# A delta-rule layer with experts: the gated output's scaling on ScalarE, the queries' square sums by products into ones, and the order around them

## The chip, the cores and the metric

One core of a Trainium2 chip runs the whole program in one launch. Its engines are TensorE (PE in the profile, its weight loads PEld), VectorE (DVE), ScalarE (ACT), GpSimd (POOL) and SyncE (SP, which here only issues DMAs). The metric is the device time of one execution in microseconds; less is better. Each engine runs its own list of instructions in order, and semaphores order the engines among themselves. All orders are written out by hand in the kernel.

## The reference

The input is 4 sequences of 512 tokens with 256 features. Two layers follow. Layer 0 adds to the tokens the sum of a gated delta-rule attention (32 value heads, 16 key heads, 128 wide) and a mixture of 64 experts; layer 1 adds a small attention over the 4 sequences and 8 experts. The part that matters here, cut down:

```python
y = conv(x @ w_qkv)                       # causal, 4 taps, per channel
q, k, v = split(silu(y))
q = q / sqrt(sum(q * q) + 1e-6) * DK ** (-0.5)
k = k / sqrt(sum(k * k) + 1e-6)
# for each token: Sm = Sm * exp(g); delta = (v - k @ Sm) * beta; Sm += outer(k, delta); o = q @ Sm
og = o * silu(z)
var = mean(og * og)
on = og * rsqrt(var + EPS) * norm_w
out = on @ w_out
```

## The kernel before, in words

`build_program` runs three parts: layer norm, gates and routing; then `heads_and_experts`, which holds the change; then the experts' combination and layer 1.

`heads_and_experts` makes 64 steps (STEPS): 16 key heads, and for each 4 chunks of 128 tokens, for all 4 sequences at once. So a tile of a step is 128 partitions by 512 columns. A step g belongs to chunk g % 4; `first_chunk` has no earlier state, so it has no `residual`, `queries_state` and `keys_state`, and `last_chunk` needs no `state_update`. The work of one chunk is spread over three steps (step g does the projections and products of chunk g, part of the triangular inverse of chunk g-1, and solves, outputs and state of chunk g-2). On the same step runs one unit of the experts (EX_IN, EX_GATE, EX_UP, EX_DOWN; in the first 8 steps GpSimd scatters tokens by indirect DMAs instead, and the experts' units begin at step 9).

The order on each engine is the function `step(g)` of its block:

- TensorE (L1002): `project` (L789) multiplies the tokens with the weights of one channel type into one of two PSUM tiles `psF`, which are used in turn in the order PLACES (L399); `slot_free` (L772) waits until ScalarE or VectorE has drained the use before. `turn_keys` (L825) and `turn_queries` (L829) transpose the keys and queries after the convolution; `products` (L837) makes k·k and q·k; `solve`, `within`, `state_update` (L935 to L963) serve chunk g-2; `turn_out` (L965) transposes the scaled output and `project_out` (L972) multiplies it with `w_out`.
- VectorE (L1603): `conv` (L1408) makes three of the four taps of the convolution, each a multiply-add over 128x512; `key_scales` (L1436), `decayed_products` (L1453, from PSUM), `row_scales` (L1553, the inverse roots), `decays` (a scan, L1444), `pivots` (L1465, the first part of the inverse of the 16x16 blocks), `level`, `new_state`, `gather_out`.
- ScalarE (L1278): `evacuate` (L1131) drains a projection; `silu`; `squares` (L1159) reads the turned keys or queries from PSUM, with an accumulated sum of each of the 4 blocks; `w_copy` (L1236), `values` (L1183, drains the turned values), `keys_copy` (L1169), `out_squares` (L1242), `compact`, `inverse_copy`, `silu_z`, `out_turned` (L1249).
- GpSimd (L1776): `join` (L1704, the second part of the blocks' inverse, after `pivots`), `gated` (L1738, o times silu(z)), `rho_w`, `state_decay`, `normed` (L1745, the gated output times its inverse root), `hidden`, `mask`, `next_weights`, and the scatters.
- SyncE loads the decays, weights and experts and carries the blocks' DMAs. Its list is not touched.

The orders of the uses of `psF` for `filled` and `drained` (L403) are not touched either. After step 63 a tail follows in which the last chunks and the last 9 experts' units run.

## Time and profile before

| what | value |
|---|---|
| median of 3 runs | 2678.14 us (2676.47 to 2680.68) |
| the profiled execution's own time | 2679.44 us |
| its span, first to last instruction | 2677.7 us |
| TensorE, VectorE busy | 88%, 87% of the span |
| ScalarE, GpSimd busy | 67%, 53% |
| mean granted TensorE clock | 0.958 of full |

The span is the profiled execution's stretch from the first to the last instruction; its own time is 1.7 us longer, and 1.3 us above the median. Busy time is the union of an engine's instructions. A busy share says nothing about which wait ends last; for that the timelines of one step are read side by side. The page's chain of the work that ended last covers mostly the last part of the program.

### The profile page before, as it was taken

The numbers are of one execution on the slowest core, as the hardware profiler recorded it, in microseconds if no ns is written. First come the engines' busy times: TensorE is split into PE (matmuls) and PEld (weight loads), VectorE is DVE, ScalarE is ACT, GpSimd is POOL, SyncE is SP. The second block draws the span as 40 slices with busy tenths as digits, with TensorE's granted clock in tenths as the row PEclk, the third lists the DMA queues.
The fourth block names the chain that finished last, engine by engine and source line by source line (L and its number), as shares of the span: only waits on it lengthen the run. The fifth ranks groups of instructions, "written<-read, shape, count | busy, mean of one in ns | idle before, by whom it ended". The sixth has DMA issues, their size and how long they took to land. (4 is left out here: it accounts for less than half of the span.)

```text
span 2677.7 us, 74015 instructions
## 1 busy us (share of the span) xinstructions
PE 2362.6 (88%) x27695; PEld 1951.4 (73%) x27696; DVE 2326.0 (87%) x5305; ACT 1788.2 (67%) x5621; POOL 1424.9 (53%) x1368
## 2 busy tenths in 40 slices
PE   1477889999999999999999999999999999758998
PEld 1366777888787878787878787878787878635555
DVE  7677888999999999999999999999999998289996
ACT  1356767787878787878787878787877787412121
POOL 2388885555555555555555555555555555266510
PEclk8679899999999999999999999999999999869999
DMA  5232112212222222221222222212122112263311
GB/s 208 89 94 67 41 42 61 57 50 51 55 57 50 57 50 57 49 57 49 57 50 57 50 57 50 57 49 58 49 57 49 46 49 57 64 206 106 104 59 48
DMA packets 244701, 175.39 MB, mean 66 GB/s; under 512 B 152635, under 2 KB 212714, under 8 KB 243160
## 3 DMA queue, kind: packets, MB, share of 16 engines
q1 hardware_dynamic: 221543, 136.89, 19.1%
q0 software_dynamic: 12288, 24.19, 2.9%
q10 hardware_dynamic: 10512, 9.57, 1.1%
q8 instruction: 222, 3.64, 0.6%
q14 instruction: 136, 1.11, 0.1%
HBM read 126.88 MB, written 53.08 MB: 67 GB/s over the span
## 5 line engine op out<-in xcount | busy, mean ns | idle before, releaser
L1417 DVE SCALAR_TENSOR_TENSOR p_y<-p_xr,cw,p_y 128x512 f32<-128x512 f32 x768 | 760.3, 997 | 33.2 <-ACT p_y L1141 14.4
L798 PE MATMUL p_psF<-xnS,w_hl 128*128 128x512 f32 x1536 | 430.6, 416 | 20.4 <-PEq L651 11.1
L798 PEld LDWEIGHTS p_psF<-xnS,w_hl 128*128 128x128 f32 x1536 | 274.4, 192 | 85.9 <-DVE p_ATP L1461 11.4
L1710 POOL TENSOR_TENSOR p_terms<-p_U 64x512 f32<-64x512 f32 x64 | 130.8, 2043 | 335.8 <-DVE p_U L1486 335.7
L1461 DVE SCALAR_TENSOR_TENSOR p_ATP<-p_psF,p_sj,p_E 128x256 f32<-128x256 f32 x512 | 211.0, 477 | 65.8 <-PE p_psF L844 64.2
L1749 POOL TENSOR_TENSOR p_O<-p_OG,p_sm 128x512 f32<-128x512 f32 x128 | 155.7, 1239 | 195.0 <-DVE p_sm L60 171.8
L1743 POOL TENSOR_TENSOR p_OG<-p_O,p_zs 128x512 f32<-128x512 f32 x128 | 162.6, 1271 | 140.5 <-ACT p_ktok L1172 69.3
L979 PE MATMUL p_psO<-p_wout,p_ont 128*128 128x256 f32 x1024 | 235.3, 383 | 0.1
L1712 POOL TENSOR_TENSOR p_terms<-p_terms 64x256 f32<-64x256 f32 (+1 forms) x256 | 220.0, 859 | 20.1
L1138 ACT ACTIVATE p_xr<-p_psF 128x512 f32<-128x512 f32 x256 | 153.4, 599 | 93.6 <-PE p_psF L798 81.8
L813 PEld LDWEIGHTS p_psF<-w_hl,xnS 128*128 128x128 f32 x1536 | 200.1, 189 | 14.3 <-DVE p_ATP L1461 5.1
L979 PEld LDWEIGHTS p_psO<-p_wout,p_ont 128*128 128x128 f32 x1024 | 191.4, 192 | 25.2 <-ACT p_ont L1253 0.8
L1246 ACT ACTIVATE p_O<-p_OG 128x128 f32<-128x128 f32 x512 | 152.4, 308 | 82.4 <-POOL p_OG L1743 81.7
L813 PE MATMUL p_psF<-w_hl,xnS 128*128 128x256 f32 x1536 | 206.0, 284 | 0.0
L1141 ACT ACTIVATE p_y<-p_psF,cw 128x512 f32<-128x512 f32 x256 | 175.0, 684 | 0.8
L1166 ACT ACTIVATE p_y<-p_psF 128x128 f32<-128x128 f32 x512 | 137.1, 300 | 48.2 <-PE p_psF L822 48.2
L822 PE MATMUL p_psF<-ident,p_kq 128*128 128x128 f32 x512 | 86.1, 292 | 93.7 <-ACT p_kq L1151 93.5
L1451 DVE TENSOR_TENSOR_SCAN p_E<-p_ab,p_identr 128x512 f32<-128x512 f32 x128 | 160.6, 1255 | 8.2 <-DMA p_ab<-decays 8.2
L1966 POOL DMA_INDIRECT w_hl<-expert_out,slot_u x96 | 100.8, 1050 | 86.9 <-DVE acc L2211 36.2
L1189 ACT ACTIVATE p_vs<-p_psF,p_vsc 128x128 f32<-128x128 f32 x512 | 146.2, 379 | 0.0
L822 PEld LDWEIGHTS p_psF<-ident,p_kq 128*128 128x128 f32 x512 | 54.8, 143 | 124.1 <-ACT p_kq L1151 124.1
L844 PE MATMUL p_psF<-p_kq 128*128 128x256 f32 x512 | 138.1, 395 | 5.5 <-ACT p_y L1166 5.5
(337 smaller groups left out, 6153.8 us busy)
## 6 DMA issues: line engine op xcount, KB each, us to landing
p_ab<-decays SPq DMA_DIRECT2D x64, 512.0 KB, 5.5
w_raw<-in_w_in SPq DMA_DIRECT2D x16, 768.0 KB, 4.0
p_wgu<-in_w_gu SPq DMA_DIRECT2D x60, 176.0 KB
expert_out<-p_ye ACTq DMA_DIRECT2D x73, 128.0 KB, 1.7
expert_in<-p_zero SPq DMA_DIRECT2D x16, 512.0 KB, 7.5
blocks_out<-p_ATc SPq DMA_DIRECT2D x64, 128.0 KB
p_DTc<-blocks_back SPq DMA_DIRECT2D x64, 128.0 KB
p_xe<-expert_in SPq DMA_DIRECT2D x60, 128.0 KB
```

Source lines behind the costliest of these rows:

```text
L798: m = pe.matmul(b4(psF[f % 2][:, :]), w_hl[:, wp, kt, ty * P:(ty + 1) * P], xnS[:, xp, kt, :].rearrange("p (b t) -> p b t", b=B)[:, :, c * ...
L813: m = pe.matmul(psF[f % 2][:, (b % 2) * 2 * P:(b % 2 + 1) * 2 * P], xnS[:, xp, kt, b * S + c * P:b * S + (c + 1) * P], w_hl[:, wp, kt, 4 * ...
L979: m = pe.matmul(psOO[:, b * D:(b + 1) * D], ont[:, v, b, :], wout[:, v, :], start=(v == 0), stop=(v == 1))
L1138: act.activation(xr[:, ty, :, TAPS - 1:], b4(psF[f % 2][:, :]), ACT.Copy)
L1141: act.activation(y[:, ty, :, :], b4(psF[f % 2][:, :]), ACT.Copy, scale=cw[:, ty, TAPS - 1:TAPS]).then_inc(s["drained"], 1)
L1246: m = act.activation(O1[:, v, b, :], OG[:, v, b, :], ACT.Square, accum_out=so[:, v, b:b + 1])
L1417: m = dve.scalar_tensor_tensor(y[:, ty, :, :], xr[:, ty, :, tap:tap + P], cw[:, ty, tap:tap + 1], y[:, ty, :, :], ALU.mult, ALU.add)
L1451: dve.tensor_tensor_scan(flat(E[:, v, :, :]), flat(ab[:, v, :, :]), flat(identr[:, :, :]), 0.0, ALU.mult, ALU.add).then_inc(s["scan"], 1)
L1461: m = dve.scalar_tensor_tensor(ATP[g % 2][:, v, b, :, :], psF[f % 2][:, (b % 2) * 2 * P:(b % 2 + 1) * 2 * P].rearrange("p (u t) -> p u t", ...
L1712: link(pool.tensor_tensor(terms[:, 0:k, :, :], terms[:, 0:k, :, :], terms[:, k:2 * k, :, :], ALU.add))
L1743: pool.tensor_tensor(OG[:, v, :, :], O1[:, v, :, :], zs[g % 2][:, v, :, :], ALU.mult).then_inc(s["og"], 1)
L1749: pool.tensor_tensor(O1[:, v, :, :], OG[:, v, :, :], over(sm[:, 1, 1 + v, :]), ALU.mult).then_inc(s["on"], 1)
```

## The change

- `normed` moves from GpSimd (two tensor-tensor products of 128x512) to ScalarE (eight ACTIVATEs of 128x128 with a per-partition scale), behind `evacuate(g, 2)`.
- The queries' square sums: instead of transposing the queries on TensorE and squaring them from PSUM with an accumulated sum, ScalarE squares the queries in place (one ACTIVATE of 128x512, `query_squares`), TensorE multiplies each of the 4 blocks into a column of ones (`query_norms`), and ScalarE copies the 128x4 sums (`query_sums`).
- The key scales: a tensor-scalar and a tensor-tensor become two scalar-tensor-tensor instructions, with a tile of 1e-6 and a factor of 1.
- Orders. ScalarE: `silu(g, 1)` ahead of `values(g-1, 0)` and `keys_copy`; `level5` ahead of `silu(g-1, 2)`; `normed`, then `inverse_copy`; `spread`, `halves` and `inverse_copy(g-1, 5)` ahead of `silu(g, 3)`. TensorE: EX_IN ahead of `within(g-2, 1)`; `state_update(g-2, 1)` behind `level_y`; `project(g, 2)` ahead of `level_x`; EX_UP ahead of `turn_out`. VectorE: both `history` and both `decays` ahead of `pivots`; `row_scales`, `conv(g, 3)` ahead of `rows_decay` and `output_weights`. GpSimd: `gated(g-2, 1)` ahead of two scatters; `mask` ahead of `hidden`.

The tail (after step 63) gets the same orders; its lines are left out here.

```diff
--- before
+++ after
@@ -420,7 +420,7 @@
 
 
 
-PER = dict(hist=2, silu=2, silu_v0=1, silu_v1=1, kss=1, vsc=1, s_ready=1, scan=2, rho=1, atp=4,
+PER = dict(hist=2, silu=2, squared=1, silu_v0=1, silu_v1=1, kss=1, vsc=1, s_ready=1, scan=2, rho=1, atp=4,
            compact=4, masked=1, halved=2, pivoted=1, joined=1, spread=4, t5=3, tt=1,
            ks=2, r=2, qs=2, qg=2, w=2, wsb=2, wr=2, decayed=2, o=2, o1=2, su=2, st=2, og=2, so=2, rstd=1, on=2, ot=2, ont=2, outp=1, acc=1)
 PER_UNIT = dict(hh=1)
@@ -475,7 +475,8 @@
         ss = [sb(f"ss{p}", [P, 2, B]) for p in range(2)]
         sm = sb("sm", [P, 3, 3, B])
         n2 = sb("n2", [P, B])
-        scratch = sb("scratch", [P, 1])
+        floor = sb("floor", [P, B])
+        ones = sb("ones", [P, 1])
         vsc = sb("vsc", [P, B])
         sj = sb("sj", [P, B, 2])
         xq = [sb(f"xq{p}", [P, B]) for p in range(2)]
@@ -651,10 +652,12 @@
         with nc.Block() as block:
             @block.vector
             def _(dve):
-                for t in (xr[:, :, :, 0:TAPS - 1], scratch[:, :], D64X[:, :, :, :], TT[0][:, :, :, :]):
+                for t in (xr[:, :, :, 0:TAPS - 1], D64X[:, :, :, :], TT[0][:, :, :, :]):
                     dve.memset(t, 0.0).then_inc(init, 1)
+                dve.memset(ones[:, :], 1.0).then_inc(init, 1)
+                dve.memset(floor[:, :], 1e-6).then_inc(init, 1)
                 dve.tensor_copy(identr[:, :, :], ident[:, :].unsqueeze(1).to_broadcast([P, B, P])).then_inc(init, 1)
-                dve.wait_ge(init, 8)
+                dve.wait_ge(init, 9)
 
             @block.gpsimd
             def _(pool):
@@ -826,9 +829,13 @@
                 wait(pe, "silu", g, 1)
                 turn(g, KEYS_T, lambda b: kq[g % 2][:, b, K_, :])
 
-            def turn_queries(g):
-                wait(pe, "silu", g, 2)
-                turn(g, QUERIES_T, lambda b: kq[g % 2][:, b, Q_, :])
+            def query_norms(g):
+
+                slot_free(g, QUERIES_T)
+                wait(pe, "squared", g, 1)
+                for b in range(B):
+                    m = pe.matmul(psF[QUERIES_T % 2][:, b:b + 1], y[:, 1, b, :], ones[:, :], start=True, stop=True)
+                m.then_inc(s["filled"], 1)
 
             def turn_values(g, v):
                 wait(pe, ("silu_v0", "silu_v1")[v], g, 1)
@@ -1017,28 +1024,28 @@
                     solve(g - 2, 0)
                     solve(g - 2, 1)
                     within(g - 2, 0)
+                expert(g, EX_IN)
+                if g >= 2:
                     within(g - 2, 1)
-                expert(g, EX_IN)
-                turn_queries(g)
+                query_norms(g)
                 products(g, 0)
                 if g >= 2:
                     state_update(g - 2, 0)
                 products(g, 1)
-                if g >= 2:
-                    state_update(g - 2, 1)
                 project(g, 3)
                 project_z(g, (0, 1))
                 expert(g, EX_GATE)
+                project(g, 2)
                 if g >= 1:
                     level_x(g - 1, 4)
-                project(g, 2)
                 project_z(g, (2, 3))
+                expert(g, EX_UP)
                 if g >= 2:
                     turn_out(g - 2)
                 if g >= 1:
                     level_y(g - 1, 4)
-                expert(g, EX_UP)
                 if g >= 2:
+                    state_update(g - 2, 1)
                     project_out(g - 2, (0, 1))
                     project_out(g - 2, (2, 3))
                 if g >= 1:
@@ -1136,6 +1143,8 @@
                     act.wait_ge(cw_in, g // NC)
                 wait(act, "hist", g - 1, 1 + ty // 2)
                 act.activation(xr[:, ty, :, TAPS - 1:], b4(psF[f % 2][:, :]), ACT.Copy)
+                if ty == Q_:
+                    wait_filled(act, g - 1, QUERIES_T)
                 if ty >= 2:
                     wait_filled(act, g - 1, VALUES_T[ty - 2])
                 act.activation(y[:, ty, :, :], b4(psF[f % 2][:, :]), ACT.Copy, scale=cw[:, ty, TAPS - 1:TAPS]).then_inc(s["drained"], 1)
@@ -1156,15 +1165,23 @@
                 wait(act, "og", g - 2, 2)
                 act.activation(zs[g % 2][:, :, 2 * half:2 * half + 2, :], psF[f % 2][:, :].rearrange("p (b v t) -> p v b t", b=2, v=2), ACT.Silu).then_inc(s["drained"], 1)
 
-            def squares(g, u):
-
-                p, f = g % 2, (KEYS_T, QUERIES_T)[u]
-                wait_filled(act, g, f)
-                if u == 0:
-                    wait(act, "vsc", g - 2, 1)
+            def key_squares(g):
+
+                wait_filled(act, g, KEYS_T)
+                wait(act, "vsc", g - 2, 1)
                 for b in range(B):
-                    m = act.activation(y[:, u, b, :], psF[f % 2][:, b * P:(b + 1) * P], ACT.Square, accum_out=ss[p][:, u, b:b + 1])
-                m.then_inc(s["drained" if u else "kss"], 1)
+                    m = act.activation(y[:, 0, b, :], psF[KEYS_T % 2][:, b * P:(b + 1) * P], ACT.Square, accum_out=ss[g % 2][:, 0, b:b + 1])
+                m.then_inc(s["kss"], 1)
+
+            def query_squares(g):
+
+                wait(act, "silu", g, 2)
+                act.activation(y[:, 1, :, :], kq[g % 2][:, :, Q_, :], ACT.Square).then_inc(s["squared"], 1)
+
+            def query_sums(g):
+
+                wait_filled(act, g, QUERIES_T)
+                act.activation(ss[g % 2][:, 1, :], psF[QUERIES_T % 2][:, 0:B], ACT.Copy).then_inc(s["drained"], 1)
 
             def keys_copy(g):
                 wait_filled(act, g, KEYS_T)
@@ -1245,6 +1262,15 @@
                 for b in range(B):
                     m = act.activation(O1[:, v, b, :], OG[:, v, b, :], ACT.Square, accum_out=so[:, v, b:b + 1])
                 m.then_inc(s["so"], 1)
+
+            def normed(g):
+                wait(act, "rstd", g, 1)
+                wait(act, "so", g, 2)
+                for v in range(2):
+                    wait(act, "og", g, v + 1)
+                    for b in range(B):
+                        m = act.activation(O1[:, v, b, :], OG[:, v, b, :], ACT.Copy, scale=sm[:, 1, 1 + v, b:b + 1])
+                    m.then_inc(s["on"], 1)
 
             def out_turned(g, v):
                 if v == 0:
@@ -1278,9 +1304,10 @@
             def step(g):
                 if g >= 1:
                     expert(g - 1, EX_DOWN)
-                    silu(g - 1, 2)
                 if g >= 2:
                     level5(g - 2)
+                if g >= 1:
+                    silu(g - 1, 2)
                 evacuate(g, 0)
                 if g >= 2:
                     queries(g - 2, 0)
@@ -1291,16 +1318,17 @@
                 silu(g, 0)
                 if g >= 2:
                     queries(g - 2, 1)
-                squares(g, 0)
+                key_squares(g)
                 if g >= 2:
                     w_copy(g - 2, 0)
                     w_copy(g - 2, 1)
+                silu(g, 1)
                 if g >= 1:
                     values(g - 1, 0)
                 keys_copy(g)
-                silu(g, 1)
+                query_squares(g)
                 expert(g, EX_IN)
-                squares(g, 1)
+                query_sums(g)
                 if g >= 2:
                     out_squares(g - 2, 0)
                     out_squares(g - 2, 1)
@@ -1308,22 +1336,23 @@
                 silu_z(g, 0)
                 expert(g, EX_GATE)
                 compact(g)
+                evacuate(g, 2)
+                if g >= 2:
+                    normed(g - 2)
                 if g >= 1:
                     inverse_copy(g - 1, 4)
-                evacuate(g, 2)
                 silu_z(g, 1)
-                if g >= 2:
-                    out_turned(g - 2, 0)
                 if g >= 1:
                     store_expert(g - 1)
                 if g >= 2:
+                    out_turned(g - 2, 0)
                     out_turned(g - 2, 1)
                 expert(g, EX_UP)
+                if g >= 1:
+                    spread(g - 1)
+                    halves(g - 1)
+                    inverse_copy(g - 1, 5)
                 silu(g, 3)
-                if g >= 1:
-                    halves(g - 1)
-                    spread(g - 1)
-                    inverse_copy(g - 1, 5)
             for g in range(STEPS):
                 step(g)
 
@@ -1437,9 +1468,9 @@
 
                 h = 2 * (g // NC)
                 wait(dve, "kss", g, 1)
-                link(dve.tensor_scalar(sm[:, 0, 0, :], ss[g % 2][:, 0, :], 1e-6, None, ALU.add))
+                link(dve.scalar_tensor_tensor(sm[:, 0, 0, :], ss[g % 2][:, 0, :], 1.0, floor[:, :], ALU.mult, ALU.add))
                 link(dve.reciprocal(n2[:, :], sm[:, 0, 0, :]))
-                dve.tensor_tensor(sj[:, :, :], gates[:, 0, g % NC:NT:NC, h:h + 2], n2[:, :].unsqueeze(2).to_broadcast([P, B, 2]), ALU.mult).then_inc(s["s_ready"], 1)
+                dve.scalar_tensor_tensor(sj[:, :, :], gates[:, 0, g % NC:NT:NC, h:h + 2], 1.0, n2[:, :].unsqueeze(2).to_broadcast([P, B, 2]), ALU.mult, ALU.mult).then_inc(s["s_ready"], 1)
 
             def decays(g, v):
 
@@ -1601,23 +1632,23 @@
                     dve.tensor_copy(cw[:, :, :], cw_raw[:, :, :]).then_inc(cw_in, 1)
 
             def step(g):
+                if g >= 1:
+                    history(g - 1, 0)
                 decays(g, 0)
                 if g >= 3:
                     gather_out(g - 3)
-                if g >= 1:
-                    history(g - 1, 0)
                 if g >= 2:
                     residual(g - 2, 0)
                 if g >= 1:
+                    history(g - 1, 1)
+                decays(g, 1)
+                if g >= 1:
                     pivots(g - 1)
-                decays(g, 1)
                 conv(g, 0)
                 if g >= 2:
                     level6(g - 2)
                     residual(g - 2, 1)
                 conv(g, 1)
-                if g >= 1:
-                    history(g - 1, 1)
                 if g >= 2:
                     outputs(g - 2, 0)
                 key_scales(g)
@@ -1627,20 +1658,21 @@
                 decayed_products(g, 1)
                 if g >= 1:
                     turn_cores(g - 1)
-                output_weights(g)
-                rows_decay(g)
                 row_scales(g)
                 conv(g, 3)
+                next_weights(g, 0)
                 conv(g, 2)
+                rows_decay(g)
+                next_taps(g)
+                output_weights(g)
                 if g >= 1:
                     level(g - 1, 4)
-                next_taps(g)
-                next_weights(g, 0)
-                next_weights(g, 1)
                 if g >= 2:
                     new_state(g - 2, 0)
+                next_weights(g, 1)
+                next_weights(g, 2)
+                if g >= 2:
                     new_state(g - 2, 1)
-                next_weights(g, 2)
             for g in range(STEPS):
                 step(g)
 
@@ -1742,12 +1774,6 @@
                 wait_drained(pool, g, Z1)
                 pool.tensor_tensor(OG[:, v, :, :], O1[:, v, :, :], zs[g % 2][:, v, :, :], ALU.mult).then_inc(s["og"], 1)
 
-            def normed(g):
-                wait(pool, "rstd", g, 1)
-                for v in range(2):
-                    wait(pool, "og", g, v + 1)
-                    pool.tensor_tensor(O1[:, v, :, :], OG[:, v, :, :], over(sm[:, 1, 1 + v, :]), ALU.mult).then_inc(s["on"], 1)
-
             def hidden(g):
 
                 if not in_use(g, EX_UP):
@@ -1780,29 +1806,27 @@
                 if g >= 2:
                     gated(g - 2, 0)
                     rho_w(g - 2)
+                    gated(g - 2, 1)
                 scatter(g, 1)
                 scatter(g, 2)
                 if g >= 2:
-                    gated(g - 2, 1)
                     state_decay(g - 2)
                 scatter(g, 3)
                 scatter(g, 4)
                 scatter(g, 5)
                 scatter(g, 6)
-                if g >= 2:
-                    normed(g - 2)
                 scatter(g, 7)
                 scatter(g, 8)
                 next_weights(g, 0)
                 scatter(g, 9)
+                scatter(g, 10)
+                mask(g)
+                scatter(g, 11)
                 hidden(g)
-                mask(g)
-                scatter(g, 10)
-                scatter(g, 11)
                 scatter(g, 12)
                 scatter(g, 13)
+                scatter(g, 14)
                 next_weights(g, 1)
-                scatter(g, 14)
                 next_weights(g, 2)
                 scatter(g, 15)
             for g in range(STEPS):
```

## Rows read from the trace of the kernel before

**Rows 1.** The page, part 1: busy us of each engine.

```profile
PE 2362.6 (88%) x27695; PEld 1951.4 (73%) x27696; DVE 2326.0 (87%) x5305; ACT 1788.2 (67%) x5621; POOL 1424.9 (53%) x1368
```
**Rows 2.** Busy time by stage: length; busy PE, PEld, DVE, ACT, POOL; granted clock; DMA share; GB/s.

```profile
898.60:1031.69 133.09, 125.92 (x1671) 107.98 (x1665) 122.42 (x265) 106.89 (x345) 71.66 (x69) 1.00 0.22 54
```
**Rows 3.** Waits from 760 to 1720 us: total us, times, longest.

```profile
PEld p_psF L822 <- ACT p_kq L1151: 49.6, 58, 2.1
...
DVE p_ATP L1461 <- PE p_psF L844: 18.8, 43, 0.9
```
**Rows 4.** Timeline of PE: start us, length us, instruction, count, [idle before, releaser].

```profile
906.16 0.65 PE L822 MATMUL p_psF<-ident,p_kq 128*128 128x128 f32 x4 [0.24 <-ACT p_kq L1151]
906.66 1.95 PE L943 MATMUL p_psS<-p_vs,p_TT 128*128 128x128 f32 x16
908.72 2.05 PE L953 MATMUL p_psO<-p_Ws,p_ATP 128*128 128x128 f32 x16
...
911.34 0.66 PE L822 MATMUL p_psF<-ident,p_kq 128*128 128x128 f32 x4 [0.34 <-ACT p_kq L1151]
...
913.16 1.16 PE L962 MATMUL p_psS<-p_Wr,p_ktok 128*128 128x128 f32 x8 [0.30 <-POOL p_Wr L1726]
914.15 1.03 PE L844 MATMUL p_psF<-p_kq 128*128 128x256 f32 x4
...
915.83 1.63 PE L798 MATMUL p_psF<-xnS,w_hl 128*128 128x512 f32 x6
...
922.94 1.04 PE L969 MATMUL p_psO<-ident,p_O 128*128 128x128 f32 x8
...
924.59 0.67 PE L996 MATMUL p_psF<-p_xeT,p_wgu 128*88 128x128 f32 x4
...
941.52 0.66 PE L822 MATMUL p_psF<-ident,p_kq 128*128 128x128 f32 x4 [1.88 <-ACT p_kq L1151]
...
1005.65 0.66 PE L822 MATMUL p_psF<-ident,p_kq 128*128 128x128 f32 x4 [1.16 <-ACT p_kq L1151]
```
**Rows 5.** Timeline of ACT, same step.

```profile
909.14 1.14 ACT L1189 ACTIVATE p_vs<-p_psF,p_vsc 128x128 f32<-128x128 f32 x4
...
910.62 0.67 ACT L1151 ACTIVATE p_kq<-p_y 128x512 f32<-128x512 f32 x1
...
915.42 0.31 ACT L1246 ACTIVATE p_O<-p_OG 128x128 f32<-128x128 f32 x1 [1.09 <-POOL p_OG L1743]
...
915.73 0.29 ACT L1246 ACTIVATE p_O<-p_OG 128x128 f32<-128x128 f32 x1
...
921.34 0.39 ACT L1196 ACTIVATE p_Xs<-p_psI 128x256 f32<-128x256 f32 x1
...
922.31 0.69 ACT L1141 ACTIVATE p_y<-p_psF,cw 128x512 f32<-128x512 f32 x1
```
**Rows 6.** Timeline of DVE, same step; last row: ns min/median/max of line 1417.

```profile
901.50 3.26 DVE L1417 SCALAR_TENSOR_TENSOR p_y<-p_xr,cw,p_y 128x512 f32<-128x512 f32 x3 [0.25 <-ACT p_y L1141]
...
906.61 2.57 DVE L1417 SCALAR_TENSOR_TENSOR p_y<-p_xr,cw,p_y 128x512 f32<-128x512 f32 x3
...
910.93 1.20 DVE L1442 TENSOR_TENSOR p_sj<-gates,p_n 128x8 f32<-128x8 f32 x1
...
915.22 1.66 DVE L1461 SCALAR_TENSOR_TENSOR p_ATP<-p_psF,p_sj,p_E 128x256 f32<-128x256 f32 x4 [0.67 <-PE p_psF L844]
...
919.49 3.00 DVE L1417 SCALAR_TENSOR_TENSOR p_y<-p_xr,cw,p_y 128x512 f32<-128x512 f32 x2
...
L1417 DVE SCALAR_TENSOR_TENSOR p_y<-p_xr,cw,p_y x342: 717/827/1554, 768.4 to 1710.1; 128x512 f32<-128x512 f32 x171
```
**Rows 7.** Timeline of POOL, same step.

```profile
907.91 0.65 POOL L1716 TENSOR_TENSOR p_U<-p_terms 64x64 f32<-64x64 f32 x1
910.84 1.27 POOL L1743 TENSOR_TENSOR p_OG<-p_O,p_zs 128x512 f32<-128x512 f32 x1 [2.28 <-ACT p_ktok L1172]
...
919.45 2.48 POOL L1749 TENSOR_TENSOR p_O<-p_OG,p_sm 128x512 f32<-128x512 f32 x2 [2.11 <-DVE p_sm L60]
```

28 lines of the change are left out of this document (14 added, 14 removed).

## The prediction

> **What bounds the kernel now.** I read the page's busy shares first, then the busy time by stage, then the waits, and last the timelines of one step. The page gives TensorE 2362.6 us, VectorE 2326.0, ScalarE 1788.2 and GpSimd 1424.9 of the span [rows 1]. The work repeats every four steps of a head, so I take the four steps from 898.60 to 1031.69 us: in 133.09 us TensorE is busy 125.92, VectorE 122.42, ScalarE 106.89, at a granted clock of 1.00 [rows 2]. So TensorE is idle 7.17 us in four steps, and no reordering can win more than that there. The waits say where: nearly all of it ends in `turn` (line 822, keys or queries from `kq`, released by ScalarE's silu), 49.6 us of weight loads from 760 to 1720 us. VectorE waits most for the products, 18.8 us [rows 3].
>
> The timeline of the step that begins at 898.60 shows two halves [rows 4]. In the first TensorE waits 0.24 us for the turned keys, 0.34 for the queries, 0.30 for `Wr`. From `project(g, 3)` at 915.83 to the end of the step it waits for nothing. `turn_out` starts at 922.94; GpSimd's `normed` ran from 919.45 for 2.48 us, so its result was 1.0 us early [rows 4, 7]. ScalarE's order decides the first half: after the second `w_copy` it does `values(g-1, 0)` (from 909.14), the keys' copy and only then silu of the queries at 910.62 [rows 5]. That silu's input, conv(g, 1), is ready at 909.18 [rows 6], so little is lost by the order.
>
> **The change part by part.**
>
> 1. *Key scales.* The TENSOR_TENSOR of 8 elements takes 1.20 us [rows 6]. It runs beside GpSimd's `gated` (910.84 + 1.27 = 912.11) and ends with it at 912.13 [rows 6, 7]. A SCALAR_TENSOR_TENSOR beside GpSimd is slowed but doesn't wait for the end: two taps of the convolution beside `normed` take 3.00 us together [rows 6]. I price the new form at 0.2 us, between that tiny size costing nothing and the full 1.20. VectorE wins 1.0 us, but just before `decayed_products`, where it waits for the products anyway [rows 3]; this gain is worth nothing unless the products come sooner.
>
> 2. *`normed` leaves GpSimd.* conv(g, 3) loses its neighbour. A tap free of GpSimd takes at best 0.72 us [rows 6], so two taps come down from 3.00 to about 1.5: 1.5 us off VectorE, in the second half, where TensorE doesn't wait for it. What it can buy is an earlier start of the next conv(g, 0). In the steps after a last chunk that matters: the turned keys come 1.88 us late there [rows 4].
>
> 3. *`normed` on ScalarE.* Eight ACTIVATEs of 128x128. The nearest, out of the same tile, stand 0.31 us apart with their accumulator read between (915.42 to 915.73) and four from PSUM take 1.14 us [rows 5]: 2.0 to 2.5 us, taken 2.3. They stand behind `evacuate(g, 2)`, which ends at 923.00 today [rows 5], and, without the 0.36 us of `inverse_copy` ahead of it, at 922.65. So the halves are ready at 923.8 and 924.95 on today's clock. TensorE, with EX_UP (0.6 us, line 996 [rows 4]) now ahead of `turn_out`, arrives at 923.55, turns one half in 0.5 and waits for the other: 0.25 + 0.7, about **1.0 us of new idle per step** (0.6 with the short price). `inverse_copy`, `silu_z` and `out_turned` follow while TensorE does `level_y` and the moved `state_update`, so `project_out` should just get its input.
>
> 4. *Query squares.* ScalarE drops four squares from PSUM and takes one of 128x512 and a tiny copy: a small relief. TensorE gives up four transposes (the next instruction starts 0.5 us after them: 906.66 - 906.16) for four products of one column, eight records. Bounds: at the pace of full 128x128 products 8/16 of 1.95 us = 1.0, and nothing [rows 4]. I take 0.5, since the weights are full and the columns few, so this changes nothing.
>
> 5. *What it waits for.* TensorE's `query_norms` stands ahead of both `products`, and needs the squares. ScalarE's new order is silu(g, 1), `values`, `keys_copy`, `query_squares`. Silu can't start before conv(g, 1) ends. That end moves: `pivots` now stands behind `decays(g, 1)` (1.2 us), so GpSimd's `join` (today until 908.56 [rows 7]) runs 1.2 us longer beside conv(g, 0) and conv(g, 1), whose taps it slows (3.26 and 2.57 us for three, against 2.2 at best [rows 6]). I take conv(g, 1) 0.5 us later, between 0 and 1.2. Then: silu 909.9 to 910.45, values to 911.45, keys_copy to 911.95, squares to 912.6. But EX_IN on TensorE needs the PSUM slot that `values` drains (911.5), and `within(g-2, 1)` (1.0 us) is queued behind it: EX_IN to 912.0, within to 913.0. So `query_norms` starts at **913.0 instead of 911.34**, 1.65 us late. Then 0.5 + 1.0 (products 0) + 1.0 (`state_update` 0) + 0.9 (products 1) gives `project(g, 3)` at 916.4, only 0.55 later than 915.83, because `state_update(g-2, 1)` has gone from here. `project_z` behind it waits for VectorE's second `decayed_products` (products 1 end 916.55, plus 1.66 [rows 6]): 918.2 against an arrival of 917.85, another 0.35.
>
> 6. *The moved `state_update(g-2, 1)`* comes back in the second half: eight records like those at 913.16, the next instruction 1.0 us later [rows 4], of which I count 0.9, the pace beside other products.
>
> 7. *Hidden:* the histories, `rows_decay`, `spread` before `halves`, `mask` before `hidden`. All have their readers over a microsecond later, and VectorE and ScalarE have spare time in the second half once TensorE is the late one; if not, they are worth 0.2 us each. In the first eight steps GpSimd also scatters; losing `normed` (2.5 us) could help there, 0 to 2.5 a step, taken at 1 for eight steps.
>
> **The sum.** This step: 0.55 + 0.35 + 0.9 + 1.0 = +2.8 us. The next (the one with 1.88 us of lateness, of which 1.6 goes, as VectorE is earlier): +1.2. The third has no `state_update`, so it loses the delay of 1.65 directly: +2.6. The fourth has no residual and less to wait for: +2.6. Together +9.2 on 133.09. Steps 9 to 63 are 13.75 such groups: +126 us; less 8 for the early steps: +118. On the profiled execution (span 2677.7, its own time 2679.44) that is 2797; on the median shown, 1.3 us lower, **2796 us**. With every term at its low bound (conv(g, 1) not delayed, norms free, `normed` 2.0) the four steps lose 5 to 6 and the time is 2745; at the high bounds (1.2 us, 1.0 us, 2.5 us) they lose 14 and it is 2860. For this case alone the range is 2745 to 2860.
>
> **The rivals.**
>
> *VectorE's relief decides (faster).* If VectorE is what really holds the loop, 2.5 us less work a step brings conv(g, 1) to its end a microsecond sooner. Then silu, `values` and squares are done before TensorE has finished `within`, and the waits at the turned keys close: these are 0.24, 1.88 and 1.16 us [rows 4] in three steps, the third repeats the 0.24: 3.5 us in four. That is 2.6%, up to 55 us: 2625; I put it at 2640 with the early steps and `turn_out`'s wait against it. For it: VectorE is 92% busy. Against: conv(g, 0) starts only after `evacuate(g, 0)`, which TensorE paces; the point from which it decides is conv(g, 1) ending 1.0 us earlier relative to the step. Chance 0.16. A rule speaks against this rival: the Trainium skill ("GPSIMD Engine Reference", section 8, Key points) says that GpSimd shares its SBUF interfaces with VectorE and contends with VectorE instructions "with two SBUF inputs". The new form of the key scales still has two, so by that rule it wins little, and this rival would have 1.0 us a step less relief. The rows show the form matters: tensor-tensor waits to the end, the other is only slowed.
>
> *Only half of the loss (slower).* The squares come in time and only `turn_out` waits: 0.6 to 1.0 us a step, offset in the step with 1.88 us. 55 steps by 0.3 to 1.0: 2695 to 2735. Chance 0.12.
>
> *No change.* Both effects cancel, or the waits only change places: 2678. Chance 0.05.
>
> **How the numbers follow.** The forecast has 0.67, and 2796 is its value. Faster by over 0.2% (5 us, about what a measurement of this kernel can tell) is 0.16, within 0.05, slower 0.79. The range 2660 to 2855 leaves out most of the faster case (0.12) and the top (0.06).
>
> **What would show it.** In the step's timeline: a gap of 0.7 us or more before TensorE's one-column products, released by ScalarE's squares; `within(g-2, 1)` behind a gap before EX_IN; a gap before the second half of `turn_out`, released by ScalarE; the key scales at 0.2 us with a longer wait before `decayed_products`; taps of conv(g, 3) at 0.75. TensorE's idle time in four steps should rise from 7.2 to about 16 us. I am wrong if conv(g, 1) ends over 0.5 us earlier after the step's start than today's 10.6 us, or if `turn_out` doesn't wait.

## The result, and the profile after

The changed kernel takes **2834.3 us** (median of 4 runs, 2828.5 to 2835.45) against 2679.36 for the kernel before on the same chip (2676.47 to 2680.68): ratio **1.0573, 95% interval [1.0559, 1.0587]**. It is slower, by 155 us. The forecast was 2796, with the range 2660 to 2855.

The page, part 1, of the kernel after (busy us; compare [rows 1]):

```profile
PE 2440.6 (86%) x27952; PEld 1986.5 (70%) x27952; DVE 2238.2 (79%) x5306; ACT 1905.3 (67%) x5749; POOL 1218.6 (43%) x1240
```

VectorE and GpSimd did get less to do (88 and 206 us less busy). The time still rose, and TensorE is busy 78 us longer. Where the 155 us lie is read from the busy time by stage: steps 2 to 11, steps 12 to 62, and the rest. First before, then after (the last row of after is the same stretch of four steps as [rows 2]):

```profile
163.84:530.40 366.56, 322.25 (x4089) 273.19 (x4085) 310.15 (x665) 258.14 (x828) 274.60 (x266) 0.95 0.21 54
530.40:2236.48 1706.08, 1613.24 (x21213) 1385.03 (x21205) 1565.92 (x3462) 1362.21 (x4385) 910.55 (x877) 0.99 0.21 53
2236.48:2677.65 441.17, 367.58 (x1931) 247.18 (x1924) 333.39 (x902) 119.82 (x290) 174.12 (x166) 0.91 0.30 94
```

```profile
164.46:543.59 379.13, 335.77 (x4130) 281.59 (x4125) 301.67 (x672) 277.81 (x848) 248.60 (x245) 0.95 0.21 53
543.59:2387.81 1844.22, 1676.29 (x21415) 1409.67 (x21408) 1486.89 (x3451) 1453.90 (x4486) 737.26 (x774) 0.99 0.19 49
2387.81:2833.00 445.19, 367.80 (x1936) 247.42 (x1928) 332.27 (x906) 127.03 (x308) 167.01 (x160) 0.91 0.29 93
...
940.58:1084.10 143.52, 130.49 (x1689) 109.49 (x1681) 117.31 (x272) 114.07 (x352) 58.24 (x61) 1.00 0.19 50
```

The early steps lose 12.6 us, the 51 steps of the loop 138.1, the tail 4.0. Four steps take 143.52 us for 133.09: +10.4. Step by step these are +2.85, +1.13, +3.33 and +3.12 us. TensorE's idle time in them rose from 7.17 to 13.03 us, and its busy time from 125.92 to 130.49, which no step of the prediction had.

The timeline of PE, for the step that begins at 940.58 (the same step as 898.60 before, [rows 4]), and the one line of the next that answers to the 1.88 us:

```profile
948.38 0.66 PE L825 MATMUL p_psF<-ident,p_kq 128*128 128x128 f32 x4 [0.44 <-ACT p_kq L1160]
...
953.26 0.44 PE L998 MATMUL p_psF<-ident,p_xe 128*128 128x128 f32 x2 [1.16 <-ACT p_vs L1206]
953.53 1.06 PE L960 MATMUL p_psO<-p_Ws,p_ATP 128*128 128x128 f32 x8
954.43 0.95 PE L837 MATMUL p_psF<-p_ones,p_y 128*128 128x1 f32 x8
955.24 1.11 PE L851 MATMUL p_psF<-p_kq 128*128 128x256 f32 x4
...
958.10 1.67 PE L801 MATMUL p_psF<-xnS,w_hl 128*128 128x512 f32 x6
...
962.23 1.66 PE L801 MATMUL p_psF<-xnS,w_hl 128*128 128x512 f32 x6 [0.25 <-ACT p_zs L1166]
...
967.66 0.66 PE L976 MATMUL p_psO<-ident,p_O 128*128 128x128 f32 x4 [0.52 <-ACT p_O L1272]
...
968.93 1.16 PE L969 MATMUL p_psS<-p_Wr,p_ktok 128*128 128x128 f32 x8
969.93 3.62 PE L986 MATMUL p_psO<-p_wout,p_ont 128*128 128x256 f32 x16
...
984.94 0.65 PE L825 MATMUL p_psF<-ident,p_kq 128*128 128x128 f32 x4 [0.46 <-ACT p_kq L1160]
```

Three new waits stand here. EX_IN (L998) waits 1.16 us for ScalarE's `values`, with half of `within` queued behind it. `project(g, 2)` waits 0.25 us for `silu_z` (it stood behind `level_x` before). The second half of `turn_out` waits 0.52 us for `normed` (L1272). The one-column products (L837) wait for nothing, but take 0.81 us to the next instruction, where the four transposes took 0.49. The 1.88 us of the step after a last chunk is 0.46. The third of the four steps has two more: `project(g, 3)` waits 0.89 us there for VectorE's `decayed_products` (0.25 before), and `project_out` 0.38 for `out_turned`.

ScalarE, VectorE and GpSimd in the same step (compare [rows 5 to 7]):

```profile
951.54 0.63 ACT L1160 ACTIVATE p_kq<-p_y 128x512 f32<-128x512 f32 x1
952.08 1.13 ACT L1206 ACTIVATE p_vs<-p_psF,p_vsc 128x128 f32<-128x128 f32 x4
953.08 0.61 ACT L1189 ACTIVATE p_ktok<-p_psF 128x512 f32<-128x512 f32 x1
953.56 0.65 ACT L1179 ACTIVATE p_y<-p_kq 128x512 f32<-128x512 f32 x1
...
965.18 1.27 ACT L1272 ACTIVATE p_O<-p_OG,p_sm 128x128 f32<-128x128 f32 x4
...
966.35 1.27 ACT L1272 ACTIVATE p_O<-p_OG,p_sm 128x128 f32<-128x128 f32 x4
```

```profile
948.94 2.57 DVE L1448 SCALAR_TENSOR_TENSOR p_y<-p_xr,cw,p_y 128x512 f32<-128x512 f32 x3
...
953.14 1.21 DVE L1473 SCALAR_TENSOR_TENSOR p_sj<-gates,p_n 128x8 f32<-128x8 f32 x1
...
956.39 3.42 DVE L1492 SCALAR_TENSOR_TENSOR p_ATP<-p_psF,p_sj,p_E 128x256 f32<-128x256 f32 x8 [1.07 <-PE p_psF L851]
...
962.25 2.32 DVE L1448 SCALAR_TENSOR_TENSOR p_y<-p_xr,cw,p_y 128x512 f32<-128x512 f32 x3
```

```profile
953.05 1.27 POOL L1775 TENSOR_TENSOR p_OG<-p_O,p_zs 128x512 f32<-128x512 f32 x1 [2.15 <-DVE p_O L1562]
```

The silu of the queries now comes first (951.54), so `values`, which EX_IN needs, runs from 952.08. The key scales take 1.21 us in the new form too, and end at 954.35, with GpSimd's `gated` (953.05 + 1.27 = 954.32).

### The profile page after: what moved, and what is told of

The parts are those of the page before. It is cut to its first block and busy times, and to the rows that moved or that the text cites. A ratio compares the mean times of both kernels' runs of the same rounds, so it can differ in the third digit from the quotient of the medians.

```text
span 2833.0 us, 74529 instructions
## 1 busy us (share of the span) xinstructions
PE 2440.6 (86%) x27952; PEld 1986.5 (70%) x27952; DVE 2238.2 (79%) x5306; ACT 1905.3 (67%) x5749; POOL 1218.6 (43%) x1240
## 5 line engine op out<-in xcount | busy, mean ns | idle before, releaser
L1448 DVE SCALAR_TENSOR_TENSOR p_y<-p_xr,cw,p_y 128x512 f32<-128x512 f32 x768 | 685.2, 892 | 89.0 <-ACT p_y L1150 70.6
L1742 POOL TENSOR_TENSOR p_terms<-p_U 64x512 f32<-64x512 f32 x64 | 75.5, 1179 | 475.7 <-DVE p_U L1517 475.5
L816 PE MATMUL p_psF<-w_hl,xnS 128*128 128x256 f32 x1536 | 216.9, 291 | 6.9 <-DVE p_ATP L1492 3.1
L816 PEld LDWEIGHTS p_psF<-w_hl,xnS 128*128 128x128 f32 x1536 | 191.2, 190 | 35.2 <-DVE p_ATP L1492 32.4
L1727 POOL TENSOR_TENSOR p_M<-p_ATc,masks 128x256 f32<-128x256 f32 x64 | 53.4, 834 | 302.5 <-PE p_psI L864 298.1
L1272 ACT ACTIVATE p_O<-p_OG,p_sm 128x128 f32<-128x128 f32 x512 | 155.9, 390 | 2.1 <-DVE p_sm L60 1.6
L851 PE MATMUL p_psF<-p_kq 128*128 128x256 f32 x512 | 148.6, 423 | 0.0
L960 PE MATMUL p_psO<-p_Ws,p_ATP 128*128 128x128 f32 x1024 | 139.3, 280 | 5.3
L1607 DVE TENSOR_TENSOR acc<-acc,p_psO 128x1024 f32<-128x1024 f32 x64 | 78.2, 1221 | 81.2 <-PE p_psO L986 80.9
```

Source lines behind the costliest of these rows:

```text
L816: m = pe.matmul(psF[f % 2][:, (b % 2) * 2 * P:(b % 2 + 1) * 2 * P], xnS[:, xp, kt, b * S + c * P:b * S + (c + 1) * P], w_hl[:, wp, kt, 4 * ...
L1272: m = act.activation(O1[:, v, b, :], OG[:, v, b, :], ACT.Copy, scale=sm[:, 1, 1 + v, b:b + 1])
L1448: m = dve.scalar_tensor_tensor(y[:, ty, :, :], xr[:, ty, :, tap:tap + P], cw[:, ty, tap:tap + 1], y[:, ty, :, :], ALU.mult, ALU.add)
```

## The experiments

"Before" and "after" name the kernel that was edited. All ratios are to the kernel before, with their 95% interval. Three questions: which part costs the time, whether the key scales' form matters, and whether the mechanisms of the prediction are the real ones.

**1. b_form: before, with the key scales' new form alone.**

```diff
-link(dve.tensor_scalar(sm[:, 0, 0, :], ss[g % 2][:, 0, :], 1e-6, None, ALU.add))
+link(dve.scalar_tensor_tensor(sm[:, 0, 0, :], ss[g % 2][:, 0, :], 1.0, floor[:, :], ALU.mult, ALU.add))
-dve.tensor_tensor(sj, gates.., n2.., ALU.mult)
+dve.scalar_tensor_tensor(sj, gates.., 1.0, n2.., ALU.mult, ALU.mult)
```

> The kernel before with only the key scales in the new form (two scalar-tensor-tensor instructions). Theory (the second SBUF input decides, whatever the form; the changed kernel's trace has 1.21 us for it): the instruction that writes sj stays at 1.20 us and ends with GpSimd's gated product, and the time stays at 2679 us within 5. Rival (my price of 0.2 us): the instruction takes 0.2 us, VectorE waits that much longer for the products, and the time is 2670 to 2679 us.

1.0012 [0.9998, 1.0026]. Timeline of DVE:

```profile
910.39 1.20 DVE L1443 SCALAR_TENSOR_TENSOR p_sj<-gates,p_n 128x8 f32<-128x8 f32 x1
```

The same 1.20 us as the TENSOR_TENSOR in [rows 6]. The form makes no difference.

**2. b_scales_early: before, with the key scales where they don't meet GpSimd's `gated`.**

```diff
+key_scales(g)
 outputs(g - 2, 0)
-key_scales(g)
 outputs(g - 2, 1)
```

> The kernel before with key_scales ahead of outputs(g-2, 0) on VectorE, so that it runs while GpSimd is idle. Theory (the 1.20 us are a wait for GpSimd's gated product, and VectorE waits for the products anyway): the instruction takes 0.17 us, the wait ahead of decayed_products grows by about 1 us, 2672 to 2681 us. Rival (VectorE's time there counts): 2610 to 2650 us.

1.005 [1.0036, 1.0063]. Timeline of DVE:

```profile
910.80 0.17 DVE L1442 TENSOR_TENSOR p_sj<-gates,p_n 128x8 f32<-128x8 f32 x1
...
914.10 1.66 DVE L1461 SCALAR_TENSOR_TENSOR p_ATP<-p_psF,p_sj,p_E 128x256 f32<-128x256 f32 x4 [1.39 <-PE p_psF L844]
```

The same instruction before, in the step that begins at 898.60 (this one begins at 899.80):

```profile
912.89 1.66 DVE L1461 SCALAR_TENSOR_TENSOR p_ATP<-p_psF,p_sj,p_E 128x256 f32<-128x256 f32 x4 [0.17 <-PE p_psF L844]
```

The eight elements take 0.17 us alone; the other 1.03 was a wait for GpSimd. VectorE only waits longer for the products instead, 1.39 us for 0.17, and starts `decayed_products` at 14.30 us in the step for 14.29: the microsecond was hidden, as the prediction had it. The small loss is a miss: `outputs` now stands behind the key scales, and in two of the four steps TensorE waits longer for `Wr`, 0.97 us for 0.33 in the step after a last chunk and 0.51 for 0.19 in the fourth. That the order of the outputs is the cause is read from the timelines, not run by itself.

**3. b_normed_act: before, with `normed` on ScalarE alone**, behind `evacuate(g, 2)` and ahead of `silu_z(g, 1)`; TensorE's order is untouched.

```diff
 evacuate(g, 2)
+if g >= 2:
+    normed(g - 2)
 silu_z(g, 1)
```

> The kernel before with only normed moved to ScalarE, behind evacuate(g, 2) and ahead of silu_z(g, 1). Theory (turn_out becomes late): ScalarE needs 2.4 us for it, TensorE waits some 2 us more per step ahead of turn_out and project_out, of which the step with the late keys gives 1.6 back because the convolution runs free of GpSimd: 2750 to 2790 us. Rival (VectorE's relief of 1.5 us a step decides): 2620 to 2665 us.

1.0445 [1.0418, 1.0471], above what was expected. Timeline of PE and busy time by stage (the column behind the five engines is the granted clock):

```profile
951.67 0.65 PE L969 MATMUL p_psO<-ident,p_O 128*128 128x128 f32 x4 [1.11 <-ACT p_O L1255]
952.84 0.66 PE L969 MATMUL p_psO<-ident,p_O 128*128 128x128 f32 x4 [0.51 <-ACT p_O L1255]
```

```profile
951.67:953.40 1.73, 1.22 (x8) 0.84 (x8) 1.11 (x2) 1.73 (x6) 0.00 (x0) 1.00 0.21 27
953.40:956.80 3.40, 3.40 (x73) 3.04 (x73) 2.22 (x7) 2.00 (x6) 0.89 (x1) 0.51 0.25 50
```

The two waits are 1.62 us. The rest is the clock: right behind them TensorE works 3.40 us at a granted clock of 0.51, the 1.2 GHz level, where about half of the time, 1.7 us by estimate, is lost. The step takes 37.29 us for 33.72, and 1.62 + 1.7 = 3.3 is nearly all of it; a step of the same kind without such a stretch takes 35.78. From step 12 on 21 of 51 steps are hit so, for 6 before.

**4. a_normed_pool: after, with `normed` back on GpSimd, at its old place; all else as in after.**

```diff
 # ScalarE
 evacuate(g, 2)
-normed(g - 2)
 # GpSimd
 scatter(g, 6)
+normed(g - 2)
 scatter(g, 7)
```

> The changed kernel with normed back on GpSimd. Theory (normed on ScalarE costs only the 0.5 us gap inside turn_out, most of the loss is in the first half): 2795 to 2815 us. Rival (normed's move is the main loss): under 2760 us. If VectorE's relief was worth something in the changed kernel, it is slower than 2834 us.

1.0616 [1.0587, 1.0645]: a clear miss, and by its median 0.4% slower than after (1.0573 [1.0559, 1.0587]; the two intervals only touch). `turn_out`'s wait is gone and a step with a last chunk is 0.8 us shorter (35.78 for 36.57). The step behind it is the one where VectorE is late. Busy time of two such steps (behind the five engines: granted clock, DMA share, GB/s):

```profile
983.99:1023.65 39.66, 36.69 (x439) 31.54 (x432) 32.36 (x73) 26.95 (x82) 17.50 (x18) 0.91 0.22 58
1129.75:1166.24 36.49, 33.67 (x440) 28.78 (x433) 32.21 (x73) 26.89 (x82) 18.03 (x18) 1.00 0.24 64
```

In the second, at the full clock, EX_IN waits 1.90 us for 1.10 in after, and `turn_out`, which no longer waits, gives that back: 36.49 us for 36.50. So VectorE's relief by `normed` is real, and worth 0.8 us there; the expectation had left it out. But at the full clock the four steps together take 141.3 us for after's 143.5. What makes this version no faster is the clock. The first of the two has a stretch of 6.8 us at half clock, which is its 3.2 us. From step 12 on 25 of 51 steps are hit, for 10 in after, and last 47 us longer for 15, counted against the unhit steps of their kind in the two profiled executions.

**5. a_transposes: after, with the transposed queries and the squares from PSUM as before; all orders and `normed` as in after.**

```diff
 # TensorE
-query_norms(g)
+turn_queries(g)
 # ScalarE
-key_squares(g)
+squares(g, 0)
...
-query_squares(g)
 expert(g, EX_IN)
-query_sums(g)
+squares(g, 1)
```

> The changed kernel with the queries transposed on TensorE and squared from PSUM as before, all orders kept. Theory (EX_IN, and within behind it, wait for the slot that values drains, and that ends at the same moment as the squares): the transposes start where the one-column products did, only their own length (0.81 against 0.5 us) is won: 2805 to 2825 us. Rival (the chain silu, values, keys_copy, query_squares is what holds the products): 2740 to 2770 us.

1.0412 [1.0385, 1.044]: the one-column products are 1.6% of the 5.7, more than was expected. The steps are 0.43 to 0.49 us shorter each, and EX_IN's wait stays (1.20 us). Of the 0.45, 0.32 is the difference of 0.81 and 0.49; the rest isn't told apart. Of the 44 us between the two profiled executions 26 lie in steps 12 to 62 and 14.5 in steps 2 to 11.

**6. a_orders_only: after, with 4 and 5 together**, so only the orders and the key scales' form differ from before.

> The changed kernel with normed back on GpSimd and the queries transposed as before: the new orders and the new form of the key scales alone. Theory (the orders themselves make EX_IN, within and the queries late by 1 us and bring state_update into the second half, where nothing waits): about 0.4 us less per step than with the one-column products, 2780 to 2815 us. Rival (the orders suit the moved work and cost nothing by themselves): under 2720 us.

1.0394 [1.0375, 1.0412]. So **the orders alone cost 104 us, two thirds of the loss**. On top of them `normed` on ScalarE costs nothing that the ratios can tell (1.0412 against 1.0394, the intervals overlap); the one-column products cost 1.6% with it and 2.2% without. Four steps at the full clock tell more, first of this run, then of number 5:

```profile
925.74:1065.45 139.71, 127.98 (x1673) 107.75 (x1665) 124.62 (x272) 107.87 (x344) 70.06 (x69) 1.00 0.20 51
...
774.89:916.58 141.69, 128.89 (x1672) 107.58 (x1664) 117.18 (x272) 116.10 (x376) 58.23 (x61) 1.00 0.20 50
```

Of the 10.4 us that the four steps lose, the orders are 6.6 (139.71 for 133.09), `normed` 2.0 and the one-column products 1.8 (143.52 for 141.69). In the profiled executions `normed`'s move costs 21 us from step 12 to 62 and 6 in the tail, and steps 2 to 11 give 11 back. That it costs so much less than the 4.45% of number 3 has more than one reason: from `project(g, 2)` to `turn_out` TensorE now has `level_x` and EX_UP to do as well (4.27 us in after, 962.23 to 966.50, for 2.93 before), so ScalarE has 1.3 us more, and the waits at `turn_out` are 0.52 us for 1.62. Which of the two orders is needed was not run.

**7. a_values_first: after, with `values(g-1, 0)` and `keys_copy(g)` ahead of `silu(g, 1)` again.**

```diff
-silu(g, 1)
 values(g - 1, 0)
 keys_copy(g)
+silu(g, 1)
 query_squares(g)
```

> The changed kernel with values(g-1, 0) and keys_copy(g) back ahead of silu(g, 1) on ScalarE. Theory (two chains end at the same moment, the slot for EX_IN and the squares, so taking one away leaves the other): the gap of 1.16 us ahead of EX_IN closes and one of about 1.1 us opens ahead of the one-column products; 2825 to 2840 us. Rival (EX_IN's slot is the only late thing): 2760 to 2775 us.

1.0547 [1.0526, 1.0568]. Timeline of PE:

```profile
945.97 0.44 PE L998 MATMUL p_psF<-ident,p_xe 128*128 128x128 f32 x2 [0.46 <-ACT p_vs L1206]
946.24 1.06 PE L960 MATMUL p_psO<-p_Ws,p_ATP 128*128 128x128 f32 x8
947.72 1.02 PE L837 MATMUL p_psF<-p_ones,p_y 128*128 128x1 f32 x8 [0.43 <-ACT p_y L1179]
```

The wait before EX_IN falls from 1.16 to 0.46 us, and 0.43 comes up at the one-column products. The step keeps its length, 36.50. ScalarE's silu, values, copy and squares are one chain in either order, and TensorE waits for its end. The time, 2819.0 us, is a little below what was expected, and the gap that opened smaller. Of the 18 us between the two profiled executions 8 are fewer drops of the clock (4 steps from step 12 on for 10).

**8. b_ex_in_early: before, with `silu(g, 1)` first on ScalarE and EX_IN ahead of `within(g-2, 1)` on TensorE.**

```diff
+silu(g, 1)
 values(g - 1, 0)
 keys_copy(g)
-silu(g, 1)
...
-within(g - 2, 1)
 expert(g, EX_IN)
+within(g - 2, 1)
 turn_queries(g)
```

> The kernel before with two of the new orders alone: ScalarE's silu(g, 1) ahead of values and keys_copy, and TensorE's EX_IN ahead of within(g-2, 1). Theory of the queue behind EX_IN (step 5 of the prediction): TensorE reaches EX_IN 1.0 us earlier than in the kernel before and then waits for ScalarE's values, which now come after the silu; within(g-2, 1) is queued behind. A gap of 1.0 to 1.6 us before EX_IN, turn_queries 1.2 to 1.5 us late, time 2740 to 2760. Rival (the orders of the second half, the moved state_update among them, cost most of the 104 us that the orders lost together): this one costs under 0.4 us a step, time 2676 to 2697.

1.0164 [1.0139, 1.0189], between the two. Timeline of PE, and busy time of the same four steps:

```profile
918.85 0.44 PE L991 MATMUL p_psF<-ident,p_xe 128*128 128x128 f32 x2 [1.06 <-ACT p_vs L1190]
919.12 1.06 PE L953 MATMUL p_psO<-p_Ws,p_ATP 128*128 128x128 f32 x8
920.01 0.60 PE L822 MATMUL p_psF<-ident,p_kq 128*128 128x128 f32 x4
...
923.88 1.41 PE L798 MATMUL p_psF<-xnS,w_hl 128*128 128x512 f32 x5
```

```profile
906.50:1043.52 137.02, 126.61 (x1672) 109.74 (x1664) 124.21 (x272) 107.78 (x345) 71.10 (x69) 0.99 0.22 52
```

The wait is there, 1.06 us, as in after. But this step starts at 906.50, so `project(g, 3)` comes at 17.38 us in it for 17.23 before: the wait takes the place of those for the queries (0.34) and for `Wr` (0.30), and the step is only 0.16 us longer. The next three lose 0.9, 0.7 and 0.5 us, and the first of them in four of thirteen cases a drop of the clock as well (37.94 us for 36.3; before has three). The row above holds one; the next four steps at the full clock take 135.34 us, with TensorE busy 125.18, no more than before. It costs about half of what the queue behind EX_IN was priced at.

**9. b_second_half: before, with TensorE's new order from `products(g, 1)` on.**

```diff
 products(g, 1)
-state_update(g - 2, 1)
 project(g, 3)
...
-level_x(g - 1, 4)
 project(g, 2)
+level_x(g - 1, 4)
 project_z(g, (2, 3))
+expert(g, EX_UP)
 turn_out(g - 2)
 level_y(g - 1, 4)
-expert(g, EX_UP)
+state_update(g - 2, 1)
```

> The kernel before with TensorE's new order from products(g, 1) on alone: state_update(g-2, 1) behind level_y, project(g, 2) ahead of level_x, EX_UP ahead of turn_out. Theory (the work only moves; what is lost are waits of project_z for VectorE's decayed_products and of project(g, 2) for ScalarE, 0.1 to 0.4 us a step, against the 0.3 us at Wr that go): 2670 to 2695. Rival (the second half's order costs as much as the first's): 2715 to 2735.

1.0199 [1.0173, 1.0224]: the rival was right, this half costs as much as the first. Busy time of the four steps, and PE's timeline in the first of them:

```profile
909.71:1046.76 137.05, 128.64 (x1672) 107.56 (x1665) 123.64 (x272) 106.19 (x345) 71.75 (x69) 1.00 0.20 52
```

```profile
928.04 1.70 PE L813 MATMUL p_psF<-w_hl,xnS 128*128 128x256 f32 x12 [0.37 <-DVE p_ATP L1460]
929.58 0.60 PE L996 MATMUL p_psF<-p_xeT,p_wgu 128*88 128x128 f32 x4
930.43 1.65 PE L798 MATMUL p_psF<-xnS,w_hl 128*128 128x512 f32 x6 [0.25 <-ACT p_zs L1156]
932.01 0.75 PE L857 MATMUL p_psI<-p_Dc,p_M 32*32 32x32 f32 x64
932.69 1.70 PE L813 MATMUL p_psF<-w_hl,xnS 128*128 128x256 f32 x12
934.44 0.67 PE L996 MATMUL p_psF<-p_xeT,p_wgu 128*88 128x128 f32 x4
```

`state_update(g-2, 1)` had covered `project_z`'s wait for `decayed_products`, now 0.37 us, and `level_x` had covered that for `silu_z`, now 0.25. Idle time is only 1.2 us more in four steps, though; busy time is 2.7 more, for the same instructions. The work behind a wait, or behind another neighbour, takes longer from its start to the next: the second `project_z` 1.75 us (932.69 to 934.44), the one behind the wait 1.54, for some 1.44 before. What lengthens them (weights loaded late, a short wait for the next tile) isn't told apart here.

**10. b_pivots_late: before, with both `history` and both `decays` ahead of `pivots` on VectorE.**

```diff
+history(g - 1, 0)
 decays(g, 0)
 gather_out(g - 3)
-history(g - 1, 0)
 residual(g - 2, 0)
-pivots(g - 1)
+history(g - 1, 1)
 decays(g, 1)
+pivots(g - 1)
...
 conv(g, 1)
-history(g - 1, 1)
```

> The kernel before with VectorE's new order of the first half alone (both histories and both decays ahead of pivots). Step 5 of the prediction had GpSimd's join run 1.2 us longer beside conv(g, 0) and conv(g, 1) and conv(g, 1) end 0.5 us later: time 2685 to 2705. Rival (join now starts and ends its first operation before the convolution needs the port, so nothing is lost and one history is out of the way of conv(g, 1)): 2670 to 2680.

0.9994 [0.9982, 1.0006]. This order alone costs nothing. Yet conv(g, 1) does end 0.35 us later, at 10.93 us in the step for 10.58, as step 5 of the prediction had it, within its 0 to 1.2: it is hidden, because the silu of the queries stands behind `values` and `keys_copy` here and starts at 12.02 (910.62 in [rows 5]). In after that silu stands first and starts at 10.96, right behind the convolution, so there the delay counts. The two orders were not run together.

**11. b_weights_early: before, with after's places for `next_weights` and `new_state` on VectorE.**

```diff
 conv(g, 3)
+next_weights(g, 0)
 conv(g, 2)
...
-next_weights(g, 0)
-next_weights(g, 1)
 new_state(g - 2, 0)
+next_weights(g, 1)
+next_weights(g, 2)
 new_state(g - 2, 1)
-next_weights(g, 2)
```

> The kernel before with the weights' casts placed as in the changed kernel (the first between conv(g, 3) and conv(g, 2), the other two together), nothing else. Theory (the third cast waits 2.2 us for GpSimd's low parts once a head, which is most of the 1.88 us that the turned keys are late in the next step): that gap falls to 0.2 to 0.5 us, 2650 to 2662 us. Rival (another wait takes its place): 2672 to 2682 us.

0.9981 [0.9972, 0.999], 2671.26 us: this one order of the change is a gain, of 4 us where at least 13 were expected, close to the rival. The turned keys wait 1.69 us in place of 1.88 in the step after a last chunk, and four steps are only 0.1 us shorter (132.97 for 133.09). In the profiled execution most of the gain is the clock: from step 12 on no step is hit, for 6 before, which is 9 us.

**12. b_vector_orders: before, with 10 and 11 together.**

> The kernel before with both of VectorE's new orders: the histories and decays ahead of pivots, and next_weights and new_state spread over the second half. Each alone gave 0.9994 and 0.9981. Theory that they act at different places (the convolution of the first half, the start of conv(g, 0) in the step after a last chunk): the gains add, 0.996 to 0.9985, 2666 to 2673. Rival (both only shift the same wait for the turned keys, or the history ahead of decays undoes the relief): 0.999 to 1.001.

0.9996 [0.9987, 1.0004]: the gains don't add. The best version stays number 11, ahead of both kernels by a little.

**The ledger.** The orders are 3.94%. Numbers 8 to 11 multiply to 1.0164 x 1.0199 x 0.9994 x 0.9981 = 1.034; the other 0.5% lies in the orders not tried alone (ScalarE's `spread`, `halves`, `level5`, GpSimd's) or in their meeting. At the full clock numbers 8 and 9 are 2.2 and 4.0 of the 6.6 us that the orders cost in four steps. The products into ones add 1.6%, `normed` on ScalarE 2.0 us in four steps, and in the whole time nothing that the ratios can tell. The key scales' form: nothing.

## Why the prediction was right or wrong

The direction and the main mechanisms were right: slower, by four steps that lose 10.4 us where 9.2 was forecast. The forecast of +118 us was 37 short. Of the four steps the first two came as forecast (+2.85 for +2.8, +1.13 for +1.2), the others were short (+3.33 and +3.12 for +2.6 each). Point by point:

- *Key scales (step 1).* Wrong price: 0.2 us was taken, 1.20 to 1.21 measured, with the old form and the new. The reading failed, not the row: two taps of 3.00 us beside `normed` were taken for "slowed, not waiting". Read one by one, the taps last 1.55 and 1.41 us for the next one's 0.75, and GpSimd's second product, started while the first tap ran, 1.49 us for the first one's 1.04: they take turns and wait for each other. The Trainium skill ("GPSIMD Engine Reference", section 8, Key points) makes no difference between the forms; by that rule the new one wins nothing, and the runs agree (1.20 and 1.20 us, 0.17 without the neighbour). The Trainium skill ("SBUF — State Buffer", section "SBUF: two separate sides") calls it an exclusive lock held for the whole instruction; the end at 954.35 beside 954.32 agrees. As the gain was counted at nothing, the sum didn't suffer.
- *`normed` off GpSimd (step 2).* Right in the duration: three taps take 2.32 us, and VectorE is 5.1 us less busy in four steps. That the 1.88 us shrank to 0.46 is only in part its work. In the step after a last chunk conv(g, 1) ends at 13.06 us before, at 11.89 with the orders alone (number 6) and at 10.86 in after. Number 4 shows what the move is worth: 0.8 us at EX_IN in that step.
- *`normed` on ScalarE (step 3).* The duration was right (2.44 us, priced 2.3); the wait was 0.52 us, not 1.0. The working had left out that `level_x` now stands behind `project(g, 2)`: TensorE arrives 0.7 us later for it (963.82 to 964.50), so the first half was in time. `project_out` was to "just get its input"; in the third step it waits 0.38 us. Number 3 shows how much hung on the orders around it, and on the clock.
- *One-column products (step 4).* The term that failed: priced 0.5 us and "changes nothing", they take 0.81 and cost 1.6%. Eight records of 0.1 us each come nearly to the pace of full products, the upper bound of 1.0; with full weights, few columns saved little, and the transposes were four records.
- *The chain to `query_norms` (step 5).* Right in place and sign. conv(g, 1) ended at 10.93 us in the step for 10.58 (0.35 late, priced 0.5; number 10 alone gives the same 10.93), EX_IN waited 1.16, `within` behind it. The products started at 13.85 us (954.43), not at 14.4, without the gap of 0.7 us that was to show them waiting: the squares were done at 954.21. `project(g, 3)` came at 17.52, not 17.8, and `project_z` waited 0.09, not 0.35. These sizes were too high by 0.1 to 0.6 us. In the third step the wait for `decayed_products` falls on `project(g, 3)` and is 0.89 us, for 0.25 before, which the forecast of +2.6 did not have.
- *The moved `state_update` (step 6).* Right: 1.0 us to the next instruction (968.93 to 969.93), priced 0.9. What it and `level_x` had covered was only half seen: the 0.25 us at `project(g, 2)` was named nowhere, and the extra busy time was not priced at all. It is 4.6 us in four steps: 2.1 from the orders (127.98 in number 6 for 125.92), 0.9 from `normed`'s move (128.89 in number 5) and 1.6 from the one-column products (130.49). Idle time rose by 5.9 us where about 9 was forecast. Two errors of opposite sign left the sum nearly right, which was luck.
- *Early steps (step 7).* Wrong sign: -1 us a step was forecast for the first eight; steps 2 to 11 cost 12.6. By the same stretch of numbers 5 and 6, `normed`'s move did win time there, 11 us, but the orders lost 9 and the one-column products 14.5. Why they cost so much beside the scatters wasn't looked into.
- *The clock.* Not in the prediction. The stretches at 0.51 to 0.53 are more frequent in after; a step with one takes 38.15 us for 36.50. From step 12 on, ten steps are hit for six before, some 5 us.

Of the rivals, *VectorE's relief decides* named a real effect, but its condition, conv(g, 1) ending 1.0 us earlier in the step, came only in the step after a last chunk (2.2 us earlier); in the other three it ended 0.3 to 0.4 later. *Only half of the loss* is refuted by EX_IN's wait, and by numbers 6 and 8.

The 37 us that the forecast was short lie so: in steps 2 to 11 about -1 was forecast (-8, and 2.3 for each of three steps), +12.6 measured; in steps 12 to 62 it was 51 x 2.3 = 117 for 138.1, of which 16 are the four steps' 10.4 for 9.2 and 5 the clock; from step 63 on 2 for 4.0.

## What to carry to other kernels

Where one engine is busy 95% of a loop's time, an order that moves a piece of its work away from a place where it covered another engine's latency costs twice: the wait that it uncovers, and longer instructions around it. Before moving work, write down what each piece covers, and price the order separately from the change of engine: here the orders were two thirds of the loss, and the move of `normed`, 4.45% alone, cost 2.0 us in four steps, and nothing that the ratios can tell, once TensorE had other work ahead of `turn_out`. Compare steps at the same clock before reading a cause from a total: number 4 lost by the clock what it had won in its steps. A tiny instruction can last a microsecond: look at what ends at the same moment on the neighbour engine before giving it another form.
